# A graph layer with experts: the transposes of the next token block, and where they stand in TensorE's program

## The chip, the core and the metric

The kernel is one program on one core of a Trainium2 chip. The metric is the device time of one execution in microseconds (us). The engines are named as the profile does: PE is TensorE's matmuls, PEld its weight loads, DVE the vector engine, ACT the scalar engine, POOL GpSimd, SP the sync engine, which issues transfers.

## The reference, cut to what matters

Input are 12500 nodes of 256 features in float32 and 200000 edges with weights, sorted by destination. Two graph convolutions are followed by a mixture of eight experts.

```
h  = layernorm(x)
h  = relu(gcn(h, W1, b1));  h = relu(gcn(h, W2, b2));  x = x + h
t  = layernorm(x)                                  # the tokens
combine = top-2 softmax weights of  t @ router_w.T, else 0
out = t
for e in range(8):
    y   = gelu(t @ w1[e] + b1[e]) @ w2[e] + b2[e]
    out = out + combine[:, e:e+1] * y
return x + out
# gcn: segment_sum(dinv[src]*ew*dinv[dst] * (h @ W)[src], dst) + dinv^2 * (h @ W) + b
```

## The kernel before

**Work.** The nodes are 98 blocks of 128 (`NB`). The edges are cut into 392 groups (`NG`) of 512, four tiles of 128 edges each (`GT`). For one tile GpSimd issues an indirect transfer (line 485) that fetches the 256 features of 128 source nodes from a table in device memory into `msg`; VectorE builds a selection matrix `sel` of 128 edges by 96 destination columns (`selection`, line 1137). In `group` TensorE multiplies the four `msg` tiles of a group by their `sel` tiles, in `products` (line 840: 8 matmuls, 16 records), into the PSUM bank `part[n % 2]`. VectorE adds the result to the sums in `accbuf` (`add`, line 1145). There are 5 groups' buffers for `msg` (`MR`) and 4 for `sel` (`R`); GpSimd waits with the messages of a group until the group five before it has been multiplied.

**Stages.** Up to about 340 us the edges are sorted into tiles and the first table is made. Layer 1 runs up to about 2240 us. Layer 2 and the experts follow: 98 iterations of four groups each. In iteration `i` the sums of one block become complete. One iteration later this block is `s`: `sums(1, s)` transposes it (line 774), VectorE makes `x2` from it (`linear`, `residual`), takes its mean and variance (`moments`) and the inverse root by three steps (`newton`, lines 1219 to 1221, the second and third behind turn 1), and writes the normalized block `tok` (`token`, line 1226). TensorE turns `tok` into `psT` (`turn_tok`, line 807: two transposes), the scalar engine copies that to `tokS` (`token`, line 593), and TensorE computes the eight router logits (`logits`, line 815), which VectorE reads (`router`, line 1236). One iteration later still the block is `last` and goes through the experts: `hidden(last, e)` (line 825, 8 records of 128 columns), GeLU on the scalar engine (line 606), `project(last, e)` (line 834, 4 records of 256 columns), and VectorE adds the share of the expert (`share`, line 1261) and its bias (`bias`, line 1273).

**Order.** Every engine runs its own program, written out by hand, and they meet at semaphores only. `turn_tok` waits for `s_tok` (the block written), for `s_tokC` and `s_lgD` (`psT` free again). In the same way `project(last, e)` waits until `share(last, e - 2)` has read its bank, and `logits` for the copy on the scalar engine. The vector engine's program holds, between the four `turn`s (an `add`, then a `selection`), the pieces of `s` and `last`:

```
turn(1); share(last, 3); newton; newton; token(s); share(last, 4)
bias(last, 4); bias(last, 5); start_sum(s); turn(2); share(last, 5); router(s)
```

and the scalar engine's holds `gelu(last, 6)`, then `token(s)`, then `gelu(last, 7)`.

Of the kernel before, what the change touches and what calls it, by code (L numbers as in the profile page):

```python
# [20 lines left out]
R = 4  # L21
# [33 lines left out]
def build(nc, x, src, dst, ew, gw1, gb1, gw2, gb2, rw, ew1, eb1, ew2, eb2, out):  # L55
# [156 lines left out]
    def sums_of(l, n):  # L212
        return wide[n % len(wide)] if l == 0 else part[n % 2]
# [104 lines left out]
    def words(eng, ap, n, low, high, why="they were worked out of node numbers below N, within these bounds"):  # L318
        _, v = nc.values_load_multi_w_load_instructions(ap, engines=[eng.engine], min_val=low, max_val=high,
                                                        skip_runtime_bounds_check_because=why)  # L320
        return v[0:n]
# [36 lines left out]
    def wait(eng, s, count):  # L358
        if not isinstance(count, int):
            eng.wait_ge(s, count)  # L360
        elif count > 0:
            eng.wait_ge(s, count)

    def stand(eng, slot):
        if not isinstance(slot.k, int):
            hold(eng)
# [298 lines left out]
    def _(pe):  # L665
# [97 lines left out]
        def sums(l, s):  # L763
            pe.wait_ge(s_agg[l], s.k)
            wait(pe, s_linD[l], s.k - 1)
            if l == 0:
                wait(pe, s_y2, s.k - 1)
            stand(pe, s)
            for k in range(KD):
                if l == 0:  # L770
                    m = pe.matmul(ps_lin, aggS[:, k, :], gw[0][:, k, :], start=(k == 0), stop=(k == KD - 1))
                else:

                    m = pe.transpose(ps_lin[:, k * P:(k + 1) * P], aggS[:, k, :], ident[:, :])
            m.then_inc(s_lin[l], 1)
# [25 lines left out]
        def turn_tok(s):  # L801
            pe.wait_ge(s_tok, s.k)
            wait(pe, s_tokC, s.k - 1)
            wait(pe, s_lgD, s.k - 1)
            stand(pe, s)
            for k in range(KD):
                t = pe.transpose(psT[:, k * P:(k + 1) * P], tok[:, k * P:(k + 1) * P], ident[:, :])  # L807
            t.then_inc(s_tokT, 1)

        def logits(s):  # L810
            pe.wait_ge(s_tokC, s.k)
            wait(pe, s_lgD, s.k - 1)
            stand(pe, s)
            for k in range(KD):
                m = pe.matmul(ps_lg, tokS[s.u][:, k, :], rwT[:, k, :], start=(k == 0), stop=(k == KD - 1))  # L815
            m.then_inc(s_lg, 1)

        def hidden(s, e):
            if e == 0:
                pe.wait_ge(s_tokC, s.k)  # L820
            wait(pe, s_gelu, (s.k - 1) * NEXP + e - 1)
            stand(pe, s)
            for m in range(KD):
                for k in range(KD):
                    mm = pe.matmul(psH[e % 2][:, m * P:(m + 1) * P], w1_s[:, e, k, m * P:(m + 1) * P], tokS[s.u][:, k, :],  # L825
                                   start=(k == 0), stop=(k == KD - 1))
            mm.then_inc(s_h, 1)

        def project(s, e):
            pe.wait_ge(s_gelu, (s.k - 1) * NEXP + e + 1)  # L830
            wait(pe, s_yadd, (s.k - 1) * NEXP + e - 1)
            stand(pe, s)
            for m in range(KD):
                mm = pe.matmul(psY[e % 2][:, 0:D], hS[:, e % 2, m, :], w2_s[:, e, m, :], start=(m == 0), stop=(m == KD - 1))  # L834
            mm.then_inc(s_y, 1)

        def products(slot, tile0, sel0):
            for h in range(KD):
                for j in range(GT):
                    m = pe.matmul(slot[:, h * W:(h + 1) * W], msg[:, tile0 + j, h * P:(h + 1) * P], sel[:, sel0 + j, :],  # L840
                                  start=(j == 0), stop=(j == GT - 1))
            return m

        def group(l, n):
            q, r = l * NG + n, n % R
            m = q % MR
            if l == 0 and n % 2 == 0:

                pe.wait_ge(s_msg[(q + 1) % MR], ((q + 1) // MR + 1) * (16 * GT))
            pe.wait_ge(s_msg[m], (q // MR + 1) * (16 * GT))  # L850

            pe.wait_ge(s_sel, q + 1)
            if l == 1:
                pe.wait_ge(s_added, q - 1)
            products(sums_of(l, n), m * GT, r * GT).then_inc(s_part, 1)
# [54 lines left out]
        for i in range(NI + 2):  # L910
            s = Slot(i, i % 2) if 0 < i <= NI else None
            g = i < NI
            if last:
                hidden(last, 0)
                hidden(last, 1)
            if g:
                group(1, R * i)
            if last:
                project(last, 0)
                hidden(last, 2)  # L920
            if s:
                sums(1, s)
            if last:
                project(last, 1)
                hidden(last, 3)
                project(last, 2)
                hidden(last, 4)
            if g:
                group(1, R * i + 1)
            if last:  # L930
                project(last, 3)
                hidden(last, 5)
                project(last, 4)
                hidden(last, 6)
            if s:
                turn_tok(s)
            if g:
                group(1, R * i + 2)
            if last:
                project(last, 5)  # L940
                hidden(last, 7)
            if s:
                logits(s)
            if last:
                project(last, 6)
            if g:
                group(1, R * i + 3)
            if last:
                project(last, 7)
            last = s  # L950
# [460 lines left out]
```

## Time and profile before

| | us |
|---|---|
| median of 3 runs (lowest, highest) | 4470.57 (4467.15, 4471.99) |
| the profiled execution, its own time | 4468.36 |
| its span, from the first to the last instruction | 4466.6 |
| PE / PEld busy | 3671.5 (82%) / 3437.6 (77%) |
| DVE busy | 2554.7 (57%) |
| ACT busy | 773.6 (17%) |
| POOL busy | 3036.1 (68%) |

The shares are means over stages that differ: the page's slices show PE at six tenths and a granted clock of eight tenths in layer 1, and both at nine or more from 2240 us on. A timeline gives the start of an instruction or of a run of like instructions, its duration, and in brackets how long its engine sat idle before it and what ended that. A matmul's end is modelled and overlaps the start of the next one, so that the text counts from start to start.

### The profile page before, as it was taken

What the parts mean: (1) busy time and instruction counts of PE and PEld (TensorE: products, weight loads), DVE (VectorE), ACT (ScalarE), POOL (GpSimd) and SP (SyncE); (2) the same over time, 40 slices, a digit from 0 to 9 for tenths busy, and PEclk for the clock granted to TensorE, in tenths of its full rate; (3) what the DMA queues carried; (4) which work ended last, traced back from release to release, by engine and by line L of the source; (5) the groups of instructions that cost most, each with busy time, mean ns of one, the idle gap of its engine ahead of it and who ended that gap; (6) DMA issues with size and microseconds to landing.
All of it is one profiled execution on the core that took longest, in us unless ns stands there. A gap on an engine that the chain in (4) does not pass through costs nothing.

```text
span 4466.6 us, 79360 instructions
## 1 busy us (share of the span) xinstructions
PE 3671.5 (82%) x27380; PEld 3437.6 (77%) x27381; DVE 2554.7 (57%) x8924; ACT 773.6 (17%) x2385; POOL 3036.1 (68%) x3196
## 2 busy tenths in 40 slices
PE   6856666666666666666599999999999999999999
PEld 5646666666666556656589999999999999999999
DVE  7623333232232323333268888888888888888887
ACT  1300000000000000000012222222222222222222
POOL 2167777777777777777677666666666666666663
PEclk9978888888888888888789999999999999999999
DMA  6343333333333333333433333333333333333332
GB/s 147 109 143 112 112 112 111 112 111 112 111 112 112 111 112 111 112 112 111 109 113 112 106 106 106 105 105 105 106 106 106 106 106 106 107 106 107 106 106 59
DMA packets 243150, 489.19 MB, mean 110 GB/s; under 512 B 60006, under 2 KB 141225, under 8 KB 242748
## 3 DMA queue, kind: packets, MB, share of 16 engines
q0 software_dynamic: 150528, 411.24, 32.6%
q1 hardware_dynamic: 84424, 66.74, 4.9%
q10 hardware_dynamic: 7796, 6.06, 0.5%
q8 instruction: 226, 3.70, 0.3%
q14 instruction: 176, 1.44, 0.1%
HBM read 445.14 MB, written 38.67 MB: 108 GB/s over the span
## 4 chain that ended last, share of the span: by engine, by line
PE 45%; POOL 32%; issue 12%; DVE 7%; DMA 3%; ACT 0%; DVEq 0%; SPq 0%; ACTq 0%; POOLq 0%
POOL msg L485 31%; PE part L840 16%; PE psH L825 12%; PE psY L834 12%; DVE sel L1137 2%; DMA msg<-ytab,srcT 2%; DVE work L1226 1%; DVE nt L1219 1%; PE psT L807 1%; PE psH L840 1%; DVE work L1261 1%; DMA ytab<-msg 1%; PE psT L815 1%; PE psY L710 1%; DVE rs L1221 1%
## 5 line engine op out<-in xcount | busy, mean ns | idle before, releaser
L485 POOL DMA_INDIRECT msg<-ytab,srcT x3136 | 2988.1, 953 | 1270.8 <-issue 894.8
L840 PE MATMUL part<-sel,msg 128*128 128x96 f32 x8384 | 1120.2, 294 | 244.0 <-DMA msg<-ytab,srcT 244.0
L840 PEld LDWEIGHTS part<-sel,msg 128*128 128x128 f32 x8384 | 1094.1, 211 | 271.2 <-DMA msg<-ytab,srcT 226.4
L825 PEld LDWEIGHTS psH<-work,wbuf 128*128 128x128 f32 x6272 | 809.6, 192 | 35.4
L1137 DVE TENSOR_SCALAR sel<-iota,relT,ewT 128x96 f32<-128x96 f32 x3136 | 835.6, 341 | 2.2 <-ACT accbuf L557 1.3
L834 PE MATMUL psY<-wbuf,work 128*128 128x256 f32 x3136 | 824.8, 386 | 0.0
L825 PE MATMUL psH<-work,wbuf 128*128 128x128 f32 x6272 | 812.4, 275 | 0.0
L606 ACT ACTIVATE work<-psH,b_s 128x128 f32<-128x128 f32 x1568 | 491.1, 364 | 1582.5 <-PE psH L825 1582.5
L1145 DVE TENSOR_TENSOR accbuf<-accbuf,part 128x192 f32 x524 | 184.8, 353 | 716.5 <-PE part L840 716.4
L834 PEld LDWEIGHTS psY<-wbuf,work 128*128 128x128 f32 x3136 | 535.9, 191 | 40.6 <-ACT work L606 0.3
L840 PE MATMUL psH<-sel,msg 128*128 128x96 f32 x2080 | 356.0, 352 | 208.0 <-DMA msg<-ytab,srcT 208.0
L840 PE MATMUL psY<-sel,msg 128*128 128x96 f32 x2080 | 358.8, 354 | 200.1 <-DMA msg<-ytab,srcT 200.1
L840 PEld LDWEIGHTS psH<-sel,msg 128*128 128x128 f32 x2080 | 345.2, 264 | 228.7 <-DMA msg<-ytab,srcT 228.7
L840 PEld LDWEIGHTS psY<-sel,msg 128*128 128x128 f32 x2080 | 348.0, 266 | 220.8 <-DMA msg<-ytab,srcT 220.8
L1261 DVE SCALAR_TENSOR_TENSOR work<-psY,comb,work 128x256 f32<-128x256 f32 x686 | 327.9, 478 | 21.7 <-PE psY L834 7.2
L1145 DVE TENSOR_TENSOR accbuf<-accbuf,psH 128x192 f32 x130 | 46.0, 354 | 458.8 <-PE psH L840 458.7
L1145 DVE TENSOR_TENSOR accbuf<-accbuf,psY 128x192 f32 x130 | 46.0, 354 | 453.8 <-PE psY L840 453.8
L1273 DVE SCALAR_TENSOR_TENSOR work<-gw,comb,work 128x256 f32<-128x256 f32 x392 | 190.4, 486 | 45.6 <-issue 34.3
L586 ACT ACTIVATE accbuf<-psT 128x256 f32 x98 | 37.7, 384 | 973.1 <-PE psT L798 973.1
L572 ACT ACTIVATE work<-psT 128x256 f32<-128x256 f32 x98 | 37.6, 384 | 718.8 <-PE psT L782 718.8
L790 PE MATMUL psG<-gw,work 128*128 128x256 f32 x392 | 110.8, 405 | 46.4 <-ACT work L572 46.4
L790 PEld LDWEIGHTS psG<-gw,work 128*128 128x128 f32 x392 | 66.4, 189 | 74.7 <-ACT work L572 69.6
(190 smaller groups left out, 2241.0 us busy)
## 6 DMA issues: line engine op xcount, KB each, us to landing
msg<-ytab,srcT POOLq DMA_INDIRECT x3136
ytab<-xS SPq DMA_DIRECT2D x99, 128.0 KB, 1.9
ytab<-msg SPq DMA_DIRECT2D x98, 128.0 KB, 1.8
xS<-in_x SPq DMA_DIRECT2D x98, 128.0 KB
out<-res SPq DMA_DIRECT2D x98, 128.0 KB
accbuf<-in_x SPq DMA_DIRECT2D x97, 128.0 KB, 3.1
wbuf<-in_L_ffn_w ACTq DMA_DIRECT2D x2, 2048.0 KB, 14.9
wbuf<-in_dst SPq DMA_DIRECT2D x1, 588.0 KB
```

Source lines behind the costliest of these rows:

```text
L485: pool.indirect_dma_start(msg[:, r * GT + j, :], None, ytab[l], bass.IndirectOffsetOnAxis(ap=srcT[:, g * GT + j:g * GT + j + 1].bitcast(U3 ...
L606: g = act.activation(hS[:, e % 2, m, :], psH[e % 2][:, m * P:(m + 1) * P], ACT.Gelu, bias=b1_s[:, e, m:m + 1])
L710: m = pe.matmul(wbanks[t // SB][0:LO, at_col:at_col + HI], wlo[:, h, r * GT + k, :], whi[:, h, r * GT + k, :], start=(k == 0), stop=(k == ...
L790: m = pe.matmul(ps_tab, h1T[:, k, :], gw[1][:, k, :], start=(k == 0), stop=(k == KD - 1))
L807: t = pe.transpose(psT[:, k * P:(k + 1) * P], tok[:, k * P:(k + 1) * P], ident[:, :])
L825: mm = pe.matmul(psH[e % 2][:, m * P:(m + 1) * P], w1_s[:, e, k, m * P:(m + 1) * P], tokS[s.u][:, k, :], start=(k == 0), stop=(k == KD - 1))
L834: mm = pe.matmul(psY[e % 2][:, 0:D], hS[:, e % 2, m, :], w2_s[:, e, m, :], start=(m == 0), stop=(m == KD - 1))
L840: m = pe.matmul(slot[:, h * W:(h + 1) * W], msg[:, tile0 + j, h * P:(h + 1) * P], sel[:, sel0 + j, :], start=(j == 0), stop=(j == GT - 1))
L1137: t = v.tensor_scalar(sel[:, r * GT + j, :], iota[:, 0:W], relT[:, g * GT + j:g * GT + j + 1], ewT[:, g * GT + j:g * GT + j + 1], ALU.is_e ...
L1145: v.tensor_tensor(to, to, sums_of(q // NG, q % NG)[:, 0:KD * W].rearrange("p (k w) -> p k w", k=KD), ALU.add).then_inc(s_added, 1)
L1261: v.scalar_tensor_tensor((front if e < NEXP - 1 else res)[s.u][:, :], psY[e % 2][:, 0:D], comb[s.u][:, e:e + 1], front[s.u][:, :], ALU.mul ...
L1273: v.scalar_tensor_tensor(front[s.u][:, :], b2_s[e][:, :], comb[s.u][:, e:e + 1], front[s.u][:, :], ALU.mult, ALU.add).then_inc(s_bias, 1)
```

## The change

In the program of TensorE for layer 2, `turn_tok(s)` is called behind group 2 of an iteration and no longer in front of it.

```
@@ -932,10 +932,10 @@
                 hidden(last, 5)
                 project(last, 4)
                 hidden(last, 6)
-            if s:
-                turn_tok(s)
             if g:
                 group(1, R * i + 2)
+            if s:
+                turn_tok(s)
             if last:
                 project(last, 5)
                 hidden(last, 7)
```

On TensorE, iteration 2 and all up to 97 have this between `hidden(last, 6)` and `project(last, 6)` before the change (L807 is `turn_tok`, L840 the group, L834 a `project`, L825 a `hidden`, L815 the logits; the loads of weights are left out):

```order
L825 MATMUL psH<-work,wbuf 128x128 x4
L807 MATMUL psT<-ident,work 128x128 x2
L840 MATMUL part<-sel,msg 128x96 x8
L834 MATMUL psY<-wbuf,work 128x256 x2
L825 MATMUL psH<-work,wbuf 128x128 x4
L815 MATMUL psT<-rwT,work 128x8 x2
L834 MATMUL psY<-wbuf,work 128x256 x2
```

And this with the change:

```order
L825 MATMUL psH<-work,wbuf 128x128 x4
L840 MATMUL part<-sel,msg 128x96 x8
L807 MATMUL psT<-ident,work 128x128 x2
L834 MATMUL psY<-wbuf,work 128x256 x2
L825 MATMUL psH<-work,wbuf 128x128 x4
L815 MATMUL psT<-rwT,work 128x8 x2
L834 MATMUL psY<-wbuf,work 128x256 x2
```

The two transposes have changed places with the eight products of the group; one `project` and one `hidden` stand between them and the logits, where the group stood there too.

In iteration 1 there is no `last` yet. TensorE has there, before the change:

```order
L774 MATMUL psG<-ident,work 128x128 x2
L840 MATMUL part<-sel,msg 128x96 x8
L807 MATMUL psT<-ident,work 128x128 x2
L840 MATMUL part<-sel,msg 128x96 x8
L815 MATMUL psT<-rwT,work 128x8 x2
L840 MATMUL part<-sel,msg 128x96 x8
```

And with the change:

```order
L774 MATMUL psG<-ident,work 128x128 x2
L840 MATMUL part<-sel,msg 128x96 x16
L807 MATMUL psT<-ident,work 128x128 x2
L815 MATMUL psT<-rwT,work 128x8 x2
L840 MATMUL part<-sel,msg 128x96 x8
```

Groups 1 and 2 now stand in a row, and the logits directly behind the transposes. The programs of the other engines are the same as before, instruction by instruction.

## Rows read from the trace of the kernel before

**Rows 1.** Busy time by stretch, layer 2: us (instructions) of each engine, clock, DMA share, GB/s.

```profile
2290.00:4405.00 2115.00, 2089.64 (x15744) 1994.68 (x15743) 1722.84 (x6088) 551.62 (x1783) 1440.31 (x1507) 1.00 0.37 107
```

**Rows 2.** Waits, 2290 to 4405: who <- for whom, total us, times, longest.

```profile
POOL msg L485 <- PE part L840: 267.7, 179, 1.8
DVE accbuf L1145 <- PE part L840: 205.3, 277, 1.8
PEld psT L807 <- DVE work L1226: 43.2, 94, 0.7
...
DVE lg L1236 <- PE psT L815: 29.8, 92, 0.3
```

**Rows 3.** Timeline of TensorE in one iteration: start us, duration us, instruction, records, idle.

```profile
3312.30 1.03 PE L834 MATMUL psY<-wbuf,work 128*128 128x256 f32 x4
...
3318.47 1.05 PE L825 MATMUL psH<-work,wbuf 128*128 128x128 f32 x8
3319.86 0.44 PE L807 MATMUL psT<-ident,work 128*128 128x128 f32 x2 [0.35 <-DVE work L1226]
3320.14 1.92 PE L840 MATMUL part<-sel,msg 128*128 128x96 f32 x16
3321.90 1.05 PE L834 MATMUL psY<-wbuf,work 128*128 128x256 f32 x4
...
3323.68 0.51 PE L815 MATMUL psT<-rwT,work 128*128 128x8 f32 x4
```

**Rows 4.** Timeline of TensorE, the last iteration with messages.

```profile
4403.10 1.92 PE L840 MATMUL part<-sel,msg 128*128 128x96 f32 x16
...
4415.93 0.38 PE L774 MATMUL psG<-ident,work 128*128 128x128 f32 x2
4416.15 1.03 PE L834 MATMUL psY<-wbuf,work 128*128 128x256 f32 x4
...
4424.07 1.05 PE L825 MATMUL psH<-work,wbuf 128*128 128x128 f32 x8
4424.96 0.38 PE L807 MATMUL psT<-ident,work 128*128 128x128 f32 x2
4425.18 1.03 PE L840 MATMUL part<-sel,msg 128*128 128x96 f32 x8
```

**Rows 5.** Timeline of VectorE in the iteration of rows 3.

```profile
3310.80 0.47 DVE L1261 SCALAR_TENSOR_TENSOR work<-psY,comb,work 128x256 f32<-128x256 f32 x1
...
3319.16 0.65 DVE L1226 TENSOR_SCALAR work<-work,mv,rs 128x256 f32<-128x256 f32 x1
...
3321.22 0.42 DVE L1231 TENSOR_TENSOR work<-work 128x256 f32<-128x256 f32 x1
3322.20 0.35 DVE L1145 TENSOR_TENSOR accbuf<-accbuf,part 128x192 f32 x1 [0.55 <-PE part L840]
```

**Rows 6.** Durations of lines 1226 and 1137: ns min/median/max, first and last start.

```profile
L1226 DVE TENSOR_SCALAR work<-work,mv,rs x98: 411/638/654, 2256.1 to 4442.9; 128x256 f32<-128x256 f32 x98
...
L1137 DVE TENSOR_SCALAR sel<-iota,relT,ewT x1504: 310/324/556, 2293.6 to 4411.0; 128x96 f32<-128x96 f32 x188
```

**Rows 7.** Timeline of TensorE, the first iterations of layer 2.

```profile
2249.57 3.73 PE L840 MATMUL part<-sel,msg 128*128 128x96 f32 x16 [0.91 <-DMA msg<-ytab,srcT]
2256.57 0.69 PE L807 MATMUL psT<-ident,work 128*128 128x128 f32 x2 [3.26 <-DVE work L1226]
...
2261.18 3.71 PE L840 MATMUL part<-sel,msg 128*128 128x96 f32 x16
...
2281.29 1.92 PE L840 MATMUL part<-sel,msg 128*128 128x96 f32 x16
```

**Rows 8.** Busy time by stretch at the start of layer 2 (columns of rows 1).

```profile
2265.00:2268.00 3.00, 3.00 (x16) 3.00 (x16) 2.13 (x10) 0.63 (x2) 2.30 (x3) 0.50 0.37 117
2268.00:2272.00 4.00, 4.00 (x33) 3.90 (x33) 3.67 (x10) 1.03 (x4) 3.04 (x3) 0.98 0.36 100
```

**Rows 9.** Timeline of the scalar engine, the copy of the transposed block.

```profile
3320.34 0.38 ACT L593 ACTIVATE work<-psT 128x256 f32<-128x256 f32 x1 [0.16 <-PE psT L807]
```

More of the change, by code:

```diff
@@ L934, in _ @@
                 hidden(last, 6)
+            if g:
+                group(1, R * i + 2)
             if s:
                 turn_tok(s)
-            if g:
-                group(1, R * i + 2)
             if last:
```

## The prediction

> **What bounds the kernel now.** I read the busy shares by stage first. From 2290 to 4405 us, which is layer 2 with the experts, TensorE is busy for 2089.64 of 2115 us at a granted clock of 1.00, VectorE for 1722.84 and GpSimd for 1440.31 [rows 1]. So what TensorE executes sets this stage, and a change there can give back only TensorE's own pauses, or add to them. The change touches nothing before 2240 us.
>
> The waits of the same stretch say what the pauses are [rows 2]. TensorE waits for one thing only: the transposes of line 807 (`turn_tok`) wait for the token block that VectorE writes in line 1226, 94 times, 43.2 us in all on the weight-load side. TensorE never waits for messages. VectorE waits for TensorE, 205.3 us before its adds and 29.8 us before it reads the logits, and GpSimd waits for a buffer that a group frees, 267.7 us.
>
> Then one iteration in order of time [rows 3]. `hidden(last, 6)` starts at 3318.47, the transposes at 3319.86, group 2 at 3320.14, `project(last, 5)` at 3321.90, the logits at 3323.68. Without a wait TensorE goes from the start of a `hidden` to the start of what follows in 0.89 us, as 4424.07 to 4424.96 shows [rows 4]; here it took 1.39. VectorE finishes line 1226 at 3319.16 + 0.65 = 3319.81 [rows 5], just in front of the transposes. That is the wait, 0.50 us.
>
> **The change, part by part.** Nothing is added or removed: two transposes and their wait go behind the 16 matmul records of group 2, in iterations 1 to 97. In iteration 98 there is no group and the order stays. No DMA, no queue and no other engine's program moves.
>
> *The wait.* With the change group 2 starts where the transposes would have started unhindered, 3318.47 + 0.89 = 3319.36. It lasts 1.76 us to the start of what follows (3320.14 to 3321.90 [rows 3]), so the transposes come at 3321.12. The token block has been ready since 3319.81: the wait is gone, with 1.31 us to spare. Line 1226 takes 411 ns in some iterations and about 650 in others (median 638 [rows 6]); this is why the wait is sometimes 0.28 and sometimes 0.51 us, and both lie inside what is spare.
>
> *The transposes themselves.* Two of them in front of group 2 cost 0.28 us when they waited (3319.86 to 3320.14) and 0.22 when they did not (4424.96 to 4425.18); in front of a `project` two transposes without a wait cost 0.22 as well (4415.93 to 4416.15) [rows 3, 4]. I take 0.22. The order group, transposes, `project` does not occur in the trace, so this has bounds: 0.22 from the row nearest to it, and 0.28 with a further 0.1 (about one matmul record of a group, 1.76 / 16 = 0.11) if the transposes start later behind a group than behind a `hidden`.
>
> *The sum for the steady part.* From the start of group 2 at 2281.29 [rows 7] to that at 4403.10 [rows 4] there are 94 iterations: (4403.10 - 2281.29) / 94 = 22.573 us each. The next one, 4403.10 to 4425.18, is the only one with messages, products and experts but no wait for the token (there VectorE had no more selections to build): 22.08 us. The changed order has the same pieces and no wait, so I take 22.08. That is 22.573 - 22.08 = 0.493 us, times 94 = 46.3 us, and about 0.3 for the one wait ahead of 2281.29: 46.6. With the other bound (0.16 more for each of 95) it is 46.6 - 15.2 = 31.4.
>
> *The first iteration.* Groups 0 and 1 wait for messages; group 1 starts at 2249.57 after waiting 0.91. Then the transposes wait 3.26 us for the token, until 2256.57, and group 3 starts at 2261.18 [rows 7]. With the change group 2 waits for its messages instead, about 2254.5 (a group's four issues take GpSimd 4.9 us, see below), and runs while VectorE finishes the token. Group 3 then waits for its own messages, until about 2259.5: some 1.6 us earlier. TensorE is granted 0.50 of its clock there, and 0.98 from about 2268 [rows 8]. If it rises at the same moment as before, half of the 1.6 us is kept, 0.8; if it rises earlier with the work, all. I take 1.0, with an end of about -2 if the rise came later instead. The Trainium skill ("TensorE: Matmul & The Clock Gate", Part 1) says that the throttled clock is the default and that sustained activity releases it; the rise at 2268 behind busy stretches agrees, and no row says when it would come here.
>
> *What is behind the moved step.* Each has its cover:
> - The scalar engine's copy of the transposed block (line 593) ended 0.86 us after the transposes began (3320.34 + 0.38 - 3319.86 [rows 9]). Now it ends at 3321.12 + 0.86 = 3321.98. The logits need it at 3319.36 + 1.76 + 0.22 + 1.78 (3321.90 to 3323.68) = 3323.12. Spare: 1.14 us. Without that cover, every us by which the copy were late would be paid in full.
> - The last GeLU, which is queued behind that copy on its engine, cannot start before `hidden(last, 7)` has ended, which is later than the copy. It costs nothing.
> - VectorE adds group 2's sums at 3322.20, behind a free moment from 3321.22 + 0.42 = 3321.64 [rows 5]. Group 2 will end before that, so the add starts at about 3321.65, 0.55 earlier, while the logits come 0.56 earlier. VectorE arrives in front of the logits as early as before, relative to them.
> - VectorE's own work is 22.573 less its waits, (205.3 + 29.8) / 93.7 = 2.51 [rows 2] (2115 / 22.573 = 93.7 iterations), so 20.06 us in each. It fits into 22.08.
> - GpSimd's is, counted in the same way, 22.573 - 267.7 / 93.7 = 19.7 us for the issues of four groups, 4.9 each. It fits as well.
> - The nearest thing that TensorE could wait for next is `share(last, 0)`, which must have read its bank before `project(last, 2)`: it ends at 3310.80 + 0.47 = 3311.27 against 3312.30 [rows 5, 3], 1.03 us spare, and both ends of that pair move together.
>
> **Sum.** 46.6 + 1.0 = 47.6 us. The profiled execution took 4468.36 us (span 4466.6): 4468.36 - 47.6 = 4420.8, so **4421 us**. Against the median of the runs, 4470.57, the same step would end at 4423; the runs lie from 4467.15 to 4471.99, so these 2 us are the scatter of the measurement. A difference under 0.2%, 9 us, could not be told from none.
>
> **Rivals.**
> 1. *Part of the gain stays away* because the new order has a price of its own, or a shorter wait comes back at the logits. With the bound above, 31.4 + 1.0 = 32 us: 4436 us. For it: no row has transposes behind a group. Against it: every other neighbourhood of transposes costs 0.22 when nothing waits. 8 in 100.
> 2. *The wait only moves.* TensorE pauses at the logits for as long as it did at the transposes, because the copy on the scalar engine is late by 1.14 + 0.49 = 1.6 us. Time 4468 us. Against it: that engine is busy for about a quarter of the stretch, and the GeLU in front of the copy ends before the transposes do. 3 in 100.
> 3. *VectorE becomes the bound, and the kernel slower.* The selections (line 1137, 16 an iteration) take 324 ns at the median and up to 556 [rows 6], and line 1226 has the same habit. If the 0.55 us by which the work of turn 2 moves against GpSimd's issues stretched all 16 by 0.23 us, VectorE would need 20.06 + 3.7 = 23.8 us an iteration: 1.2 us over today's period, 94 times, 113 us slower, 4581. It is slower than before from 11 stretched selections on (2.51 / 0.23). Against it: the median shows that most are short today, where GpSimd issues in most of the stretch, and only the four of turn 2 move against it. 2 in 100. The Trainium skill ("SBUF — State Buffer", "SBUF: two separate sides") states that VectorE in a mode with two ports and GpSimd take one port pair in turns, each for a whole instruction. By that rule the stretched ones would be those that meet an issue; the trace does show both lengths, but not that this is what parts them.
>
> **Numbers.** The forecast has 87 in 100. Its range takes in the first iteration's ends and half of the way to the dearer transposes; the range that holds 8 in 10 is 4415 to 4432 us. Faster by over 0.2%: 0.94 (forecast and rival 1, less a little). Within 0.2%: 0.03. Slower: 0.03.
>
> **What would show it.** In the changed profile: no wait of line 807 for line 1226 but the first; group 2 starts 0.89 us behind `hidden(last, 6)`, the transposes 1.76 behind group 2, `project(last, 5)` 0.22 behind them; 22.08 us from one group 2 to the next, in every iteration, with no more of the two lengths; VectorE's wait at turn 2's add gone, and that before the logits still about 0.3 us. The forecast is wrong if a wait of TensorE stands at line 815, if the period is above 22.25 us, or if the mean of line 1137 has grown.

## The result and the profile after

The changed kernel takes 4416.98 us (median of 4 runs, 4411.93 to 4420.17), the kernel before 4470.55 (4467.15 to 4471.99, also 4). The ratio is 0.9881, 95% interval 0.9866 to 0.9897, so it is faster by 1.0 to 1.3%. The forecast was 4421, the range 4415 to 4432. Not every chip gives these times: on two of the four chips on which experiments ran, the kernel before itself takes 4953 and 5006 us (experiments 5 and 6).

The profiled execution of the change took 4411.93 us, its span is 4410.1. The busy times of layer 2, by stretch (columns of [rows 1]):

```profile
2290.00:4350.00 2060.00, 2060.00 (x15694) 1983.06 (x15693) 1710.24 (x6072) 551.17 (x1774) 1441.54 (x1506) 1.00 0.38 109
```

TensorE is busy without a gap, against 2089.64 of 2115 before [rows 1]. Waits in the same stretch (who, for whom, us in total, times, longest). Left out are the scalar engine's for the products before its GeLUs, 1349.0 us, and some smaller ones; no row of TensorE is among the waits any more:

```profile
POOL msg L485 <- PE part L840: 231.2, 241, 1.9
DVE accbuf L1145 <- PE part L840: 158.1, 184, 1.9
ACT work L593 <- PE psT L807: 127.0, 94, 1.4
DVE lg L1236 <- PE psT L815: 39.2, 93, 0.5
```

The timeline of TensorE in one iteration, and the same places as in [rows 3]:

```profile
3309.00 1.05 PE L825 MATMUL psH<-work,wbuf 128*128 128x128 f32 x8
3309.89 1.92 PE L840 MATMUL part<-sel,msg 128*128 128x96 f32 x16
3311.65 0.38 PE L807 MATMUL psT<-ident,work 128*128 128x128 f32 x2
3311.87 1.03 PE L834 MATMUL psY<-wbuf,work 128*128 128x256 f32 x4
3312.73 1.05 PE L825 MATMUL psH<-work,wbuf 128*128 128x128 f32 x8
3313.62 0.51 PE L815 MATMUL psT<-rwT,work 128*128 128x8 f32 x4
...
4346.55 1.92 PE L840 MATMUL part<-sel,msg 128*128 128x96 f32 x16
...
4368.61 1.92 PE L840 MATMUL part<-sel,msg 128*128 128x96 f32 x16
```

Group 2 starts 0.89 us behind `hidden(last, 6)`, the transposes 1.76 behind the group, `project` 0.22 behind them. The last two rows are group 2 of iterations 96 and 97: 22.06 us apart. And VectorE, to be laid beside [rows 5]:

```profile
3309.70 0.65 DVE L1226 TENSOR_SCALAR work<-work,mv,rs 128x256 f32<-128x256 f32 x1
...
3311.76 0.42 DVE L1231 TENSOR_TENSOR work<-work 128x256 f32<-128x256 f32 x1
3312.10 0.35 DVE L1145 TENSOR_TENSOR accbuf<-accbuf,part 128x192 f32 x1
...
3314.17 0.17 DVE L1236 COPY lg<-psT 128x8 f32<-128x8 f32 x1 [0.37 <-PE psT L815]
```

The token block is ready at 3309.70 + 0.65 = 3310.35, and its transposes start at 3311.65: 1.30 us to spare. The add of group 2 waits no longer. VectorE waits 0.37 us before it reads the logits, a little more than before: the mean is 39.2 / 93 = 0.42 against 29.8 / 92 = 0.32 [rows 2].

**Where the 56.5 us went.** The two spans, 4466.6 and 4410.1, compared piece by piece. The start of layer 2 in the changed kernel, on TensorE:

```profile
2224.90 8.32 PE L840 MATMUL part<-sel,msg 128*128 128x96 f32 x48 [12.78 <-DMA msg<-ytab,srcT]
...
2250.43 3.73 PE L840 MATMUL part<-sel,msg 128*128 128x96 f32 x16 [1.39 <-DMA msg<-ytab,srcT]
2253.96 0.63 PE L807 MATMUL psT<-ident,work 128*128 128x128 f32 x2
2255.06 0.61 PE L815 MATMUL psT<-rwT,work 128*128 128x8 f32 x4 [0.47 <-ACT work L593]
2255.53 2.00 PE L840 MATMUL part<-sel,msg 128*128 128x96 f32 x16
...
2260.55 2.02 PE L840 MATMUL part<-sel,msg 128*128 128x96 f32 x16 [1.20 <-DMA msg<-ytab,srcT]
```

and the two rows of the kernel before that answer to its first and its last:

```profile
2229.35 7.80 PE L840 MATMUL part<-sel,msg 128*128 128x96 f32 x48 [13.02 <-DMA msg<-ytab,srcT]
...
2268.14 1.94 PE L840 MATMUL part<-sel,msg 128*128 128x96 f32 x16
```

| piece | before | after | difference |
|---|---|---|---|
| up to the first group of layer 2 | 2229.35 | 2224.90 | 4.45 |
| from there to group 0 of iteration 2 | 38.79 | 35.65 | 3.14 |
| on to group 2 of iteration 2 | 13.15 | 12.68 | 0.47 |
| 94 iterations | 2121.81 | 2073.32 | 48.49 |
| the rest | 63.50 | 63.55 | -0.05 |

(Group 2 of iteration 2 starts at 2281.29 before and at 2273.23 after.) The first piece has nothing to do with the change: the programs are the same there. The other four sum to 52.05 us.

### The profile page after: what moved, and what is told of

Read it like the earlier page. It is cut to its first block, busy times and chain, and to the rows that moved or that the text cites. A ratio compares the mean times of both kernels' runs of the same rounds, so it can differ in the third digit from the quotient of the medians.

```text
span 4410.1 us, 79360 instructions
## 1 busy us (share of the span) xinstructions
PE 3646.5 (83%) x27380; PEld 3431.6 (78%) x27381; DVE 2548.8 (58%) x8924; ACT 776.3 (18%) x2385; POOL 3039.0 (69%) x3196
## 4 chain that ended last, share of the span: by engine, by line
PE 52%; POOL 33%; issue 11%; DMA 3%; ACT 0%; DVE 0%; SPq 0%; ACTq 0%; DVEq 0%; POOLq 0%
POOL msg L485 33%; PE part L840 16%; PE psH L825 16%; PE psY L834 16%; DMA msg<-ytab,srcT 1%; PE psT L815 1%; DMA ytab<-msg 1%; PE psY L710 1%; PE psT L807 0%; PE psG L774 0%; PE psH L840 0%; PE psG L710 0%; PE part L710 0%; PE psY L840 0%; PE part L697 0%
## 5 line engine op out<-in xcount | busy, mean ns | idle before, releaser
L840 PE MATMUL part<-sel,msg 128*128 128x96 f32 x8384 | 1126.3, 295 | 252.6 <-DMA msg<-ytab,srcT 252.6
L840 PEld LDWEIGHTS part<-sel,msg 128*128 128x128 f32 x8384 | 1100.0, 212 | 280.2 <-DMA msg<-ytab,srcT 235.7
L825 PEld LDWEIGHTS psH<-work,wbuf 128*128 128x128 f32 x6272 | 808.0, 192 | 35.4
L834 PE MATMUL psY<-wbuf,work 128*128 128x256 f32 x3136 | 822.2, 385 | 0.0
L825 PE MATMUL psH<-work,wbuf 128*128 128x128 f32 x6272 | 810.7, 275 | 0.0
L834 PEld LDWEIGHTS psY<-wbuf,work 128*128 128x128 f32 x3136 | 535.7, 191 | 40.6 <-ACT work L606 0.3
L840 PE MATMUL psH<-sel,msg 128*128 128x96 f32 x2080 | 357.6, 353 | 199.4 <-DMA msg<-ytab,srcT 199.4
L840 PEld LDWEIGHTS psH<-sel,msg 128*128 128x128 f32 x2080 | 346.7, 265 | 220.1 <-DMA msg<-ytab,srcT 220.1
L840 PE MATMUL psY<-sel,msg 128*128 128x96 f32 x2080 | 351.4, 348 | 198.4 <-DMA msg<-ytab,srcT 198.4
L840 PEld LDWEIGHTS psY<-sel,msg 128*128 128x128 f32 x2080 | 340.5, 261 | 219.1 <-DMA msg<-ytab,srcT 219.1
```

## The experiments

Theory A is that of the prediction: the gain is TensorE's wait for the token block, and it is paid out as far as there is other work to fill it. Theory B: the new order is cheaper by itself, by its neighbours or because group 2 frees its buffers earlier. Experiments 1 to 4 ran on one chip, on which the kernel before takes 4466.64 us.

**1. The wait taken away without the change.** The order is the old one; the token block comes 0.69 us earlier, since one Newton step is left out of the inverse root.

```
             if s:
                 newton(s, then)
-                newton(s, then)
                 token(s)
```

> The old order, but the inverse root takes one of its three Newton steps less (the second of the two behind turn 1), so the token block is ready about 0.69 us earlier (3319.12 on the scale of the iteration shown, where TensorE is free at 3319.36). What is computed differs in the last digits of the normalization. Theory A, the gain is TensorE's wait for line 1226: the wait goes without the change, the period from one group 2 to the next is 22.08 us, the time 4420 to 4427. Theory B, the gain is the new order itself (group 2 earlier, buffers and VectorE's add earlier, or cheaper neighbours for the transposes): little or nothing, period 22.4 to 22.6, time 4455 to 4470.

Measured: 4418.15 us, ratio 0.9891 (0.9874 to 0.9907). The old order, on TensorE:

```profile
3313.62 1.05 PE L825 MATMUL psH<-work,wbuf 128*128 128x128 f32 x8
3314.51 0.38 PE L807 MATMUL psT<-ident,work 128*128 128x128 f32 x2
3314.73 1.92 PE L840 MATMUL part<-sel,msg 128*128 128x96 f32 x16
3316.49 1.06 PE L834 MATMUL psY<-wbuf,work 128*128 128x256 f32 x4
3317.39 1.05 PE L825 MATMUL psH<-work,wbuf 128*128 128x128 f32 x8
```

The transposes start 0.89 us behind `hidden`, with no wait, and the period is 22.08 or 22.09 in all steady iterations. Of the 50.5 us that the change gives on this chip (4466.64 less 4416.14, experiment 4), 48.5 are there without the new order, so theory A holds. The time is 2 us under the range that was expected. VectorE also has 0.69 us less to do here; experiments 7 and 8 move the token and leave VectorE's work alone. The 0.03 us by which the period with the change is shorter stands in the rows: behind the transposes a `project` takes 0.86 us to the next start (3311.87 to 3312.73 above), behind a group 0.90 (3316.49 to 3317.39 here). Times 94 that is 2.8 us, the size of the 2.0 by which the two times differ, and all that is seen of theory B.

**2. The transposes as late as they can go.**

```
             if last:
                 project(last, 5)
                 hidden(last, 7)
             if s:
+                turn_tok(s)
                 logits(s)
```

(and gone from behind group 2.)

> The transposes go even further back, behind hidden(last, 7) and right in front of the logits. Theory A with the copy as the next bound: the logits wait for the scalar engine's copy, which ends 0.86 us after the transposes begin, of which they cover 0.22: a new wait of 0.64 us at line 815 in each iteration, period 22.70, time 4476 to 4480, so slower than the kernel before. Theory B (what counts is that group 2 comes early): no loss against the change, 4417.

Measured: 4490.37 us, ratio 1.0053 (1.0036 to 1.0069): slower than the kernel before. TensorE and the scalar engine:

```profile
3305.57 1.05 PE L825 MATMUL psH<-work,wbuf 128*128 128x128 f32 x8
3306.47 0.38 PE L807 MATMUL psT<-ident,work 128*128 128x128 f32 x2
3307.32 0.61 PE L815 MATMUL psT<-rwT,work 128*128 128x8 f32 x4 [0.47 <-ACT work L593]
3307.79 1.11 PE L834 MATMUL psY<-wbuf,work 128*128 128x256 f32 x4
```

```profile
3306.88 0.38 ACT L593 ACTIVATE work<-psT 128x256 f32<-128x256 f32 x1 [3.13 <-PE psT L807]
```

Here is rival 2's wait: the logits start 0.85 us behind the transposes and not 0.22. The period is 22.82, 0.12 more than expected, and the time 10 us above the expected range. Of the 0.12, 0.10 is behind the wait: the logits take 0.47 to the next start, against 0.37 where nothing waited (3313.62 to 3313.99 in the changed kernel). The weight loads of the logits tell the two apart, here and in the changed kernel:

```profile
3307.32 0.52 PEld L815 LDWEIGHTS psT<-rwT,work 128*128 128x128 f32 x4 [0.71 <-ACT work L593]
```

```profile
3313.51 0.53 PEld L815 LDWEIGHTS psT<-rwT,work 128*128 128x128 f32 x4
```

Behind the wait the first load starts together with its matmul, at 3307.32; without a wait it started 0.11 us in front of it. So a wait cost 0.1 us more than itself. The place too late costs more (0.76 us an iteration) than the one too early did (0.52).

**3. Between the two.** The transposes go behind `project(last, 5)` (and are gone from behind group 2).

```
             if last:
                 project(last, 5)
+            if s:
+                turn_tok(s)
+            if last:
                 hidden(last, 7)
```

> The transposes go behind project(last, 5), so that one hidden (0.89 us) stands between them and the logits. By the copy's 0.86 us the logits wait for 0.0 to 0.1 us: 0.22 + 0.89 = 1.11 us are there to cover it, so theory A says no wait, period 22.06 to 22.10, time within 3 us of the changed kernel (4414 to 4421). If the copy came later than thought (by the last GeLU or by another queue), the wait would show at line 815 and the time would be over 4425.

Measured: 4415.49 us, ratio 0.9883 (0.9867 to 0.9900), period 22.08 or 22.09, no wait of TensorE. Both places between group 2 and `hidden(last, 7)` give the same: 4415.49 and 4416.14 (experiment 4) differ by less than either scatters. TensorE has no gap left that an order could fill.

**4. The change once more, beside these.**

> The changed kernel once more, as the measure for the three others. 4412 to 4421 us, period 22.06. It also tells the scatter of layer 1 and of the first iteration of layer 2: the profiled run of the change reached layer 2 4.4 us earlier than that of the kernel before though nothing differs there, and its clock rose about 14 us earlier. If both are scatter, at least one of them is not repeated here.

Measured: 4416.14 us (4412.69 to 4416.49), period 22.06. Its first group of layer 2 starts at 2229.57, as late as in the kernel before, and its span is 4414.4. So the 4.45 us of the table are scatter. The spans of the kernel before and of this run are 52.2 us apart, but come from two sets of runs; in this run's own set the medians are 50.5 us apart. The stretch from the first group to group 0 of iteration 2 took 35.2, 35.65, 36.3, 37.1 and 37.2 us in five profiles with the transposes behind group 2 or later (this one, the first, experiments 3, 7 and 2), and 36.45, 37.8 and 38.8 in three with the old order (experiments 1 and 8, and the kernel before). The means, 36.3 and 37.7, are 1.4 us apart, less than either kind scatters. What does not scatter as much is the start of group 3 of iteration 1, behind that first group: 30.0 to 30.8 us in the five, 31.8 in the kernel before and in experiment 8 (30.7 in experiment 1, whose token comes earlier). So the order brings that group forward by 1.0 to 1.8 us; the rest of the scatter is the clock, which has risen to 1.00 for this group in the first profile and in this one, and only 5 to 7 us after its start in the other three.

**5. and 6. On two other chips.** Four kernels ran on a chip on which the kernel before takes 4953 us, and later two on another, where it takes 5006. Two of the four write the token block later, in the changed kernel and in the kernel before (the edit is shown under 7 and 8). The other two are the changed kernel with more work for VectorE: three more Newton steps an iteration, or one, whose result nobody reads (and `CH = 40` in place of 24, for the steps' columns).

```
             if s:
                 router(s, then)
+                newton(s, then)
+                newton(s, then)
+                newton(s, then)
```

> The changed order on TensorE, and VectorE writes the token block (line 1226) behind share 4 and the biases 4 and 5 instead of in front of them, 1.6 us later, with no work added. By the changed kernel's trace the block was ready 1.3 us before its transposes (1.5 where line 1226 was short). Theory A: the spare time is used up and a wait of 0.1 to 0.35 us comes back at line 807, period 22.2 to 22.5, time 4428 to 4458. If the order itself were the gain and TensorE's distance to the token did not matter: 22.06, 4416.

> The same late token block with the old order on TensorE. Theory A: the old wait of 0.5 us grows by the full 1.6, to 2.1 us, period 24.2 us, time 4610 to 4625, so that the two orders are 160 to 190 us apart where they were 50. Theory B (each order has its own price, the wait is incidental): the two stay 50 us apart.

> The changed kernel with 2.06 us more work on VectorE in each iteration (three more Newton steps behind the router, whose result nobody reads). It measures rival 3, where VectorE becomes the bound. By the sum alone VectorE has 20.06 + 2.06 = 22.12 us to do and the time is 4422. By the places: the work comes 1.9 us late to turn 3 (it waited 0.17 there) and to share(last, 0), which had 1.1 us to spare before project(last, 2): TensorE waits about 0.8 us at line 834, period 22.9, time 4490 to 4503.

> The same with one more Newton step, 0.69 us. Both ways of counting say that it is covered (0.5 us late against 1.1 spare): period 22.06, time within 3 us of the changed kernel, 4413 to 4420. If VectorE were nearer to the bound than the trace shows, the period would be over 22.1.

Measured: 4953.83 (new order, late token; ratio 0.9997), 5169.31 (old order, late token; 1.0424), 4973.16 (VectorE with 2.06 us more; 1.0041, 1.0027 to 1.0055) and 4971.70 us (with 0.69 more; 1.0040, 1.0024 to 1.0056). The two orders are 215 us apart, where theory A had expected 160 to 190 and theory B 50. Not all of that is the wait: in layer 2 the granted clock falls to 0.50 in 70 stretches with the old order and in 3 with the new one. And 0.69 us more on VectorE, which was to be free, makes a kernel that has the change slower than the kernel before. TensorE's largest wait from 2700 to 4700 us in that kernel:

```profile
PE psY L834 <- DVE work L1261: 129.6, 79, 1.9
```

and the place, first VectorE, then TensorE:

```profile
3317.53 0.35 DVE L1145 TENSOR_TENSOR accbuf<-accbuf,part 128x192 f32 x1 [1.13 <-remote]
...
3323.92 0.35 DVE L1145 TENSOR_TENSOR accbuf<-accbuf,part 128x192 f32 x1 [1.21 <-remote]
```

```profile
3315.60 1.06 PE L834 MATMUL psY<-wbuf,work 128*128 128x256 f32 x4
...
3320.03 1.06 PE L834 MATMUL psY<-wbuf,work 128*128 128x256 f32 x4
...
3325.77 0.45 PE L834 MATMUL psY<-wbuf,work 128*128 128x256 f32 x1 [1.82 <-DVE work L1261]
```

The `project` behind a group starts at 3315.60 and 3320.03, and VectorE adds the group's sums at 3317.53 and 3323.92, 1.93 and 3.89 us later. It had been free for 1.13 and 1.21 of them (idle time in the brackets), and the profile names no releaser in this core ("remote"). In the changed kernel on the first chip the same distance, from the start behind a group to an add that waited for it, is 0.30 us (3316.69 to 3316.99). So `share(last, 0)` is late, the 1.1 us it had to spare are gone, and `project(last, 2)` waits for it. This wait is not made by the added work: the last kernel of this section shows it in the steady part of the kernel before as well, beside that for the token. What delays the signals on those chips no run tells.

Nor does this wait alone account for the loss. The usual period of this kernel is 24.14 us, but 15 of its 95 iterations take 1.6 to 3.9 us longer. Less what the iteration behind each gives back, this comes to 25 us, more than the 18.6 by which the kernel is behind. In these iterations, and in no other, the granted clock falls, nearly always just behind the pause at `project(last, 2)`. One of them, by stretch, with the pause from 2759.3 to 2761.1:

```profile
2750.00:2761.00 11.00, 9.34 (x71) 8.69 (x70) 8.14 (x28) 2.19 (x7) 6.98 (x8) 1.00 0.38 109
2761.00:2766.00 5.00, 4.90 (x26) 4.76 (x26) 3.12 (x12) 1.25 (x4) 2.48 (x3) 0.66 0.37 105
```

The kernel with three steps more has 13 such iterations, which come to 20 us, the 20.0 by which it is behind. The kernel before was not traced on this chip, so whether its clock falls here too is not shown; and the change alone was not among the runs on either slow chip, so what it gives there stays open.

The last two, on the third chip, are the three Newton steps again and a kernel that has the new place in iteration 1 alone:

```
-            if s:
+            if s and i != 1:
                 turn_tok(s)
             if g:
                 group(1, R * i + 2)
+            if s and i == 1:
+                turn_tok(s)
```

> The changed kernel with 2.06 us more work on VectorE behind the router, once more beside a kernel before of about 4467 us. By the sum alone (20.06 + 2.06 = 22.12 us) the time is 4422. By the places (share(last, 0) has 1.1 us to spare and comes 1.9 late) TensorE waits about 0.8 us at line 834, period 22.9, 4490 to 4503 us.

> The change in iteration 1 alone; all later iterations keep the old order. Theory A: the steady part stays as before, period 22.57 on the mean with the two lengths of the wait. From the first group of layer 2 to group 0 of iteration 2 it takes 35 to 36.5 us as in three runs with the change, and not 38.8 as before: 2.5 to 3.5 us of gain, 4463 to 4466 us beside a kernel before of 4467. If the start were scatter of the clock and not of the change, 38 to 39 us can come here as well and the time does not differ from before.

Measured: 5045.32 us (ratio 1.0071, 1.0055 to 1.0087) and 5007.81 us (0.9999, 0.9990 to 1.0008). The first has 27 long iterations with a fall of the clock, which come to 30 of the 39.0 us by which it is behind. The second, whose steady part is that of the kernel before (its lines stand two further down), has both waits:

```profile
PE psY L834 <- DVE work L1263: 95.2, 82, 1.5
PE psT L807 <- DVE work L1228: 61.0, 73, 0.9
```

Its usual period is 24.54 us, and its clock stays at 1.00 from 2700 to 4900 us. The gain expected of its first iteration, 2.5 to 3.5 us, is not seen, against runs that scatter by 11 and 15 us. Neither of the two decides what it was made for: how much more work VectorE could take on the first chip is not measured.

**7. and 8. The late token again,** on a fourth chip, on which the kernel before takes 4467.59 us. VectorE writes the token block later, with the same work.

```
             if s:
                 newton(s, then)
                 newton(s, then)
-                token(s)
             if last:
                 share(last, 4, 4)
                 bias(last, 4, 5)
                 bias(last, 5, 5)
             if s:
+                token(s)
                 start_sum(s)
```

> The late token block with the changed order once more, because the kernel before took 4953 us on the chip of the last four runs, 490 more than on the first, with stretches in which every engine stood, and no distance of a tenth of a us can be read there. Where the kernel before takes about 4467, theory A says a wait of 0.1 to 0.35 us at line 807, period 22.2 to 22.5, 4428 to 4458 us; the rival, 4416.

> The late token block with the old order once more. Theory A: wait 2.0 to 2.2 us, period 24.0 to 24.3, 4600 to 4625 us where the kernel before takes 4467; theory B: about 50 us more than the run beside it.

Measured: 4429.95 us with the new order (ratio 0.9917, 0.9900 to 0.9933) and 4618.92 with the old one (1.0336, 1.0318 to 1.0353): 189 us apart, where theory B had expected 50. TensorE, first the new order, then the old:

```profile
3316.11 1.05 PE L825 MATMUL psH<-work,wbuf 128*128 128x128 f32 x8
3317.00 1.92 PE L840 MATMUL part<-sel,msg 128*128 128x96 f32 x16
3318.87 0.44 PE L807 MATMUL psT<-ident,work 128*128 128x128 f32 x2
3319.15 1.03 PE L834 MATMUL psY<-wbuf,work 128*128 128x256 f32 x4
```

```profile
3316.79 1.05 PE L825 MATMUL psH<-work,wbuf 128*128 128x128 f32 x8
3319.64 0.44 PE L807 MATMUL psT<-ident,work 128*128 128x128 f32 x2 [1.79 <-DVE work L1226]
3319.91 1.92 PE L840 MATMUL part<-sel,msg 128*128 128x96 f32 x16
```

With the new order the transposes start 1.87 us behind the group, 0.11 more than unhindered, and cost 0.28 and not 0.22: period 22.22 or 22.23 in most iterations. With the old order they start 2.85 us behind `hidden` in this iteration, 1.96 too late, and 1.87 to 1.88 too late in most; the usual period is 24.01. The two periods differ by 1.78 us. That is the group of 1.76 us which the new order has in front of the wait: where both orders wait, the group hides exactly its own length; where the old one waited 0.28 or 0.51, as in the kernel before, it hides just that.

## Why the prediction was right

**The bound.** That TensorE's own work is the floor of the stage, and its only pause the wait for line 1226, was right: the pause is gone and TensorE is busy for 2060.00 of 2060.00 us; experiment 1 gets the same from the other side.

**The period.** Forecast 22.08 us, from the one iteration of the kernel before that had no wait; measured 22.06. The neighbours of the transposes cost 1.76 and 0.22 as taken, and the dear end (rival 1) did not come. The 0.02 that is left was not in the sum: a `project` right behind the transposes is 0.03 us cheaper to the next start. This term came to 48.5 us for 94 iterations against 46.3, and with the pieces at its front to 49.0 against 46.6.

**The first iteration.** Forecast 1.0 us with an end of -2 and no more than 1.6 if the clock rose earlier. In the profiled pair it gave 3.14, because both things met: group 3 started 1.2 us earlier (30.63 us behind the first group, and not 31.83) and already ran with the clock up (2.00 us for the group, and not 3.71 [rows 7]). The means over eight profiles are 1.4 apart, with more scatter than that, so that the forecast's nearness to them shows little. Group 3 did come earlier, but was not held by its messages, as the working had it: in front of it the logits, here directly behind the transposes, waited 0.47 us for the scalar engine's copy (2255.06 above), and this wait stands in all five profiles. It is the forecast's own sign of being wrong, a wait of TensorE at line 815, in one iteration of 97; the working had counted the copy's cover for the steady order alone. That the clock's rise can move by more than the work that is moved was not in the working either.

**The sum.** 47.6 forecast; 52.05 in the profiled pair without the piece that the change does not touch. The medians are 53.6 us apart there and 50.5 beside experiment 4. The remaining distance of the profiled time, 4411.93, to the forecast of 4421 is the 4.45 us by which that execution reached layer 2 earlier. The median, 4416.98, is 4 us from the forecast.

**What was to hide the moved step.** The copy on the scalar engine ended at 3312.07 + 0.38 = 3312.45:

```profile
3312.07 0.38 ACT L593 ACTIVATE work<-psT 128x256 f32<-128x256 f32 x1 [1.35 <-PE psT L807]
```

The logits came at 3313.62, 1.17 us later (forecast 1.14). Taking the `project` and the `hidden` between them away, 0.86 + 0.89 us of cover, in experiment 2 made the logits wait for the copy. The spare time in front of the transposes, forecast as 1.31 us, was 1.30, and experiment 7, which writes the token later, uses it up and shows 0.11 us of wait. VectorE's wait in front of the add went as forecast; the one before the logits, forecast as about 0.3 us, is 0.42 on the mean. The two lengths of line 1226 have gone from the period, as forecast; in the line itself they are still there (below).

**The rivals.** Rival 2's wait exists, two places further back (experiment 2) and in iteration 1. Rival 3, VectorE as the bound, did not come on the chips of the result; line 1137 kept its median of 324 ns. On the two slow chips something like it is seen: its place is the one that the prediction named as next, `share(last, 0)` before `project(last, 2)`, but what it goes with is VectorE standing idle until late signals, and not longer selections.

## What to carry to other kernels

Where the bounding engine pauses for another's result in every round of a loop, look for a piece of its own work behind the wait that does not need the result, and count two distances: from the producer to the moved step, and from it to its first reader. Both must stay positive; here they were 1.3 and 1.2 us. One place further back cost nothing (experiment 3), two places turned the gain of 1.2% into a loss of 0.5% (experiment 2). A round in the trace that happened not to wait gave the new period to 0.02 us without any model. As long as the clock stays up, a wait removed was worth at most the work that is moved in front of it.

## What was not expected of the hardware

**The length of line 1226 follows GpSimd's issues.** In the kernel before it was either 0.41 or 0.65 us. The places against the start of the last indirect transfer's issue (line 485, 0.95 us long, every 1.25) tell them apart. In experiment 1 the instruction starts 0.97 us behind an issue in most iterations (3313.63 behind 3312.66) and is short in nearly all; in experiment 7 it starts 0.67 behind and takes 0.50; in the kernel before and in the changed one it starts 0.41 to 0.42 behind, and there both lengths occur. The durations (ns min/median/max) of line 1226 in experiments 1 and 7:

```profile
L1226 DVE TENSOR_SCALAR work<-work,mv,rs x98: 410/412/469, 2253.2 to 4392.2; 128x256 f32<-128x256 f32 x98
```

```profile
L1226 DVE TENSOR_SCALAR work<-work,mv,rs x98: 406/497/575, 2248.9 to 4404.1; 128x256 f32<-128x256 f32 x98
```

The stretched ones that start 0.41 to 0.56 behind the issue's start all end 1.06 to 1.07 behind it (0.42 + 0.65). Less the 0.41 that the instruction needs, what held them was over at 0.66, before the issue's own end at 0.95. Those that start at 0.66 to 0.81 in experiments 7 and 8 take 0.50 wherever they start, and no such end fits them; the few that start up to 0.35 behind an issue, in all runs, take 0.41 or 0.42. Why some that start at 0.41 or 0.42 are not held at all, the trace doesn't tell. That the issue is what stretches the line is read from these places; no run was made without the issues. The Trainium skill ("SBUF — State Buffer", "SBUF: two separate sides") says of VectorE in a mode with two ports and GpSimd that the one which comes second blocks until the whole instruction of the other is over. Whether line 1226 is in such a mode the trace doesn't tell, and the hold that it shows is shorter than GpSimd's instruction: undisturbed ones (0.42 + 0.41 us) lie wholly inside an issue of 0.95.

**A short pause in every round can cost the clock.** In experiment 8 TensorE pauses for 1.7 to 2.0 us, mostly 1.71, in every iteration of 24.01. In eight iterations of layer 2, 11 to 15 apart, the iteration takes 25.67. One of them, by stretch:

```profile
3455.00:3464.00 9.00, 7.32 (x55) 6.81 (x53) 6.90 (x26) 2.50 (x8) 5.78 (x6) 1.00 0.31 89
3464.00:3469.00 5.00, 4.98 (x27) 4.62 (x28) 2.22 (x7) 0.38 (x1) 1.74 (x2) 0.68 0.17 51
```

Behind the pause the granted clock is 0.68 on the mean of 5 us: for part of it TensorE ran at 1.2 and not 2.4 GHz, and the iteration was 1.66 us longer. Pauses of 0.3 to 0.5 us, as the kernel before had them in every iteration, never did that: its clock was 1.00 throughout [rows 1]. Nor is it the idle time of a round alone that decides: in the kernel with the new place in iteration 1 alone TensorE stands idle for 2.0 us an iteration, in two pauses of 1.15 and 0.85, and the clock never falls, while the kernel with 0.69 us more on VectorE is idle for 1.7 us, nearly all in one pause, and loses the clock in 15 iterations. Why the clock falls in these iterations and not in the others stays open.

**The same program differs by over 10% between chips:** 4466.64 and 4467.59 us for the kernel before on two of them, 4953.12 and 5006.35 on two others, each steady within 0.4%. On a slow one VectorE, standing idle, went on 1.93 and 3.89 us after TensorE's next start in the rows shown, against 0.30 on the first; why stays open.
